# Rounding the bit-linear rows by a conversion to a scaled 16-bit float, with all five instruction orders written anew

## The reference, cut to what matters

```python
def bit_linear(x, w, b):
    gamma_x = jnp.clip(jnp.max(jnp.abs(x), axis=-1, keepdims=True), 1e-05, None)
    scale_x = 127.0 / gamma_x
    x_dq = jnp.clip(jnp.round(x * scale_x), -128.0, 127.0) / scale_x
    ...
    gamma_w = jnp.clip(jnp.mean(jnp.abs(w)), 1e-05, None)
    w_dq = jnp.clip(jnp.round(w / gamma_w), -1.0, 1.0) * gamma_w
    ...
    return jnp.einsum('bsd,hd->bsh', x_ste, w_ste) + b
gate = jax.nn.silu(bit_linear(x, gate_w, gate_b))
val = bit_linear(x, val_w, val_b)
return bit_linear(gate * val, out_w, out_b)
```

## Time and profile before

| what | value |
|---|---|
| time, median of 3 executions | 828.62 us (824.5 to 832.47) |
| span of the profiled execution | 828.8 us; its own time is not listed beside it |
| mean granted TensorE clock | 0.948 of full speed |
| instructions | 22129 |
| busy share PE / DVE / ACT / POOL | 92% / 89% / 84% / 77% |

### The profile page before, as it was taken

How to read it: one execution, slowest core, us unless ns; L and a number is a source line. 1 busy time by engine, 2 the same in 40 slices (tenths; PEclk the granted TensorE clock), 3 DMA queues, 4 the chain that set the end, 5 groups by cost and what they waited for, 6 DMA issues and landing times. The chain is left out here.

```text
span 828.8 us, 22129 instructions
## 1 busy us (share of the span) xinstructions
PE 759.6 (92%) x6898; PEld 397.6 (48%) x6898; DVE 739.1 (89%) x1636; ACT 699.6 (84%) x1447; POOL 636.2 (77%) x1139
## 2 busy tenths in 40 slices
...
GB/s 287 140 54 19 71 67 64 76 105 94 112 87 108 109 110 110 108 116 112 104 111 116 112 101 110 109 105 106 117 101 120 99 91 115 95 87 91 57 72 20
DMA packets 197952, 82.59 MB, mean 100 GB/s; under 512 B 139710, under 2 KB 196670, under 8 KB 197836
## 3 DMA queue, kind: packets, MB, share of 16 engines
...
## 5 line engine op out<-in xcount | busy, mean ns | idle before, releaser
L1141 DVE TENSOR_REDUCE mx<-psS 128x2 f32<-128x512 f32 x512 | 334.1, 680 | 21.8 <-PE psS L630 20.2
L813 ACT ACTIVATE prob<-psT 128x512 f32<-128x512 f32 x512 | 292.5, 604 | 27.0 <-PE psT L638 21.6
L630 PE MATMUL psS<-KQ 31*128 31x256 f16 x1024 | 137.6, 285 | 7.0 <-DVE mx L1141 3.6
L652 PE MATMUL psW<-prob,vst 128*32 128x256 f32 x2048 | 143.0, 400 | 0.1
L741 PE MATMUL psW<-guT,xT 128*128 128x512 bf16 x512 | 132.6, 387 | 6.2 <-DMA xT<-stage 5.3
L638 PE MATMUL psT<-KQ 32*128 32x256 f16 x1024 | 130.4, 280 | 4.0 <-ACT prob L813 3.1
L652 PEld LDWEIGHTS psW<-prob,vst 128*32 128x32 f32 x2048 | 55.0, 112 | 61.4 <-issue 34.6
L741 PEld LDWEIGHTS psW<-guT,xT 128*128 128x128 f16 x512 | 43.1, 99 | 71.5 <-issue 36.5
L1025 POOL TENSOR_TENSOR hqB<-wide,rnd 128x512 bf16<-128x512 f32 x60 | 63.1, 1056 | 13.6 <-ACT wide L863 13.4
L1039 POOL TENSOR_TENSOR stage<-stage 128x512 f16<-128x512 f32 x60 | 69.7, 1162 | 2.5 <-ACT stage L924 1.8
L630 PEld LDWEIGHTS psS<-KQ 31*128 31x128 f16 x1024 | 40.4, 93 | 64.2 <-DVE mx L1141 38.0
...
## 6 DMA issues: line engine op xcount, KB each, us to landing
...
xP<-in_x SPq DMA_DIRECT2D x32, 128.0 KB, 2.3
cP<-in_ctx SPq DMA_DIRECT2D x32, 128.0 KB, 2.1
xA<-in_x SPq DMA_DIRECT2D x32, 128.0 KB, 2.7
cB<-in_ctx SPq DMA_DIRECT2D x32, 128.0 KB, 2.3
oV<-uA SPq DMA_DIRECT2D x32, 128.0 KB, 2.1
out<-x SPq DMA_DIRECT2D x32, 128.0 KB, 2.0
...
```

The source lines that it names most:

```text
L630: m = nc.tensor.matmul(psS[:, n % 2, T * k:T * k + T], KQ[p % DEEP][r, 1, g, 128 * k:128 * k + 128], KQ[p % DEEP][r, 0, g, :], start=True, ...
L652: m = nc.tensor.matmul(bank[32 * j:32 * j + 32, :], vst[p % DEEP][:, k, 4 * n + j, :], prob[:, (4 * n + j) % 8, k, :], start=(k == 0), sto ...
L813: m = nc.scalar.activation(flat(prob[:, n % 8, :, :]), psT[:, n % 2, :], ACT.Exp, scale=float(HC) ** -0.5)
L1141: m = nc.vector.tensor_reduce(mx[:, p % 2, :, 4 * (n % 4) + n // 4], psS[:, n % 2, :].rearrange("p (c s) -> p c s", c=NK), AX.X, ALU.max)
```

## The change

- The scales become smaller by SUB = 2^24, and `xq` and `hr` write float16 (`xqB`, `hqB` are float16 now), so that ScalarE's conversion on the output does the rounding: a multiple of 2^-24. `xr` and both `hq` go, with the tiles `xrB`, `hrB` and `rnd`. The factor 2^24 comes back in the column scales.
- `tern` (the ternary weights), `xqT` and `hqT` are float16. The scale parts beside `xqB` stay bf16, through a second view `xrb`; the transposes of the last two pairs follow the types, and `lqc` becomes two copies.
- `hr` waits now for what `hq` waited for (the transpose of the pair before); `sxB` and `xnB` wait for `xq` where they waited for `xr`; `qT` and `ht` wait for `xq` and `hr`.
- All of `ORDER`, `HEAD` and `TAIL` is written anew; LOOP's bounds move by one or two. The banks are the same.

```diff
+SUB = 16777216.0
...
-    "pe": """ro:-5 pv0:-1 T6:-1 S8:0 T7:-1 bg0:-3 S9:0 proj0:2 Bg0:-3 S10:0 T8:-1 T9:-1 S11:0 pv1:-1 Bd:-4 bv0:-3
...
+    "pe": """S9:-3 pv0:-4 T8:-4 S10:-3 proj0:-1 bg0:-6 S11:-3 Bg0:-6 pv1:-4 S12:-3 T9:-4 T10:-4 Bd:-7 S13:-3 bv0:-6 Bv0:-6 bg1:-6
...
-LOOP = {"pe": (9, 26), "dve": (10, 26), "act": (10, 26), "pool": (9, 26), "sp": (9, 25)}
+LOOP = {"pe": (10, 26), "dve": (10, 26), "act": (10, 26), "pool": (10, 26), "sp": (10, 26)}
...
-        tern = [sb(f"tern{i}", [P, 2 * HID], BF16) for i in range(3)]
+        tern = [sb(f"tern{i}", [P, 2 * HID], F16) for i in range(3)]
...
-        xnB, xrB = sb("xnB", [P, T]), sb("xrB", [P, T])
-        xqB, xqT = sb("xqB", [P, T + P], BF16), sb("xqT", [P, NK + 1, P], BF16)
+        xnB = sb("xnB", [P, T])
+        xqB, xqT = sb("xqB", [P, T + P], F16), sb("xqT", [P, NK + 1, P], F16)
+        xrb, xrbT = xqB[:, T:T + P].bitcast(BF16), xqT[:, NK, :].bitcast(BF16)
...
-        hqB, hqT = sb("hqB", [P, HID], BF16), sb("hqT", [P, 8, P], BF16)
+        hqB, hqT = sb("hqB", [P, HID], F16), sb("hqT", [P, 8, P], F16)
...
                 elif name == "ht":
-                    after_apart(sp, "hq", p)
+                    after_apart(sp, "hr", p)
...
-                elif kind == "xr":
+                elif kind == "xq":
                     after(act, "sxB", p)
-                    after(act, "xq", p - 1)
-                    m = nc.scalar.activation(xrB[:], xnB[:], ACT.Copy, scale=sB[:, p % 2, 2:3], bias=ROUND)
-                elif kind == "xq":
-                    after(act, "xr", p)
                     after_late(act, p - 1, "lq", "qT")
-                    m = nc.scalar.activation(xqB[:, 0:T], xrB[:], ACT.Copy, bias=-ROUND)
+                    m = nc.scalar.activation(xqB[:, 0:T], xnB[:], ACT.Copy, scale=sB[:, p % 2, 2:3])
...
                 elif kind == "hr":
                     after(act, "sx", p)
-                    after(act, "hq", p - 1, n)
-                    m = nc.scalar.activation(hrB[:, 512 * n:512 * n + 512], hB[:, 512 * n:512 * n + 512], ACT.Copy,
-                                             scale=sB[:, p % 2, 8:9], bias=ROUND)
+                    after_late(act, p - 1, "lh", "ht", part=1)
+                    m = nc.scalar.activation(hqB[:, 512 * n:512 * n + 512], hB[:, 512 * n:512 * n + 512], ACT.Copy,
+                                             scale=sB[:, p % 2, 8:9])
...
-                elif kind == "hq":
-                    h = slice(512 * n, 512 * n + 512)
-                    after(pool, "hr", p, n)
-                    after_dma(pool, "ht", p - 1)
-                    m = nc.gpsimd.tensor_tensor(hqB[:, h], hrB[:, h], rnd[:].broadcast_to([P, 512]), ALU.subtract)
```

More of the change, by code:

```diff
@@ L72 @@
 DEEP = 3
-SET_POOL, SET_DVE = 13, DEEP + 3
+SET_POOL, SET_DVE = 12, DEEP + 3
 ORDER = {
-    "pe": """ro:-5 pv0:-1 T6:-1 S8:0 T7:-1 bg0:-3 S9:0 proj0:2 Bg0:-3 S10:0 T8:-1 T9:-1 S11:0 pv1:-1 Bd:-4 bv0:-3
[L76 to L89, removed]
```

413 lines of the change are left out of this document (212 added, 201 removed).

## The result

The changed kernel takes 889.3 us (median of 4 runs, 887.72 to 890.04), beside 828.05 us for the kernel before on the same chip: ratio 1.0715, 95% interval [1.0657, 1.0773]. I had forecast 856 us and a range from 838 to 871. Slower was right; the size was missed by 33 us. Executions of one kernel lie up to 2% apart, and the profile of three_merged, further down, is of its slowest (895.8 us, where the other three took 879.3 to 887.8).

The account below looks back on a forecast made before the run. PE and DVE bound the kernel before, PE alone after. From 828.8 us: +28.9 for pairs 5 to 25, +0.5 for pairs 26 to 30, 0 for the start, -1 for the end: 857, taken as 856, range 838 to 871.

Parts of the forecast that it names:

- PE bounds both kernels, and the change costs: Middle periods: PE and DVE both at their floor before; after, PE alone sets the period; slower 0.87.
- The price of groups: PE's score steps: 0.317 to 0.337 us a group of one to four; 16 groups for 8 cost 2.2 us a period.
- The rounding costs nothing on the path: ACT and POOL passes: xq's 13.5 us and hq's 63.1 us go, no gain from hr, operand types cost nothing.
- Neither sets the period, so none of this is on the path directly: ACT at some 19.8 and POOL at 17.1 us a period after the change, so their savings give nothing directly.
- earlier transposes: ht can start a hq (1.06 us) and a wait earlier; at most 0.77 us a period given back.
- The price of a period, 23.34 us: PE's summed distances for a period after, beside 21.16 before (21.36 measured).
- As a check I summed each instruction's undisturbed distance to its successor, by the kinds of both: PE's two orders: 21.16 us a period before, 23.34 after, difference 2.18, checking the 2.2 from groups.
- I leave 0.3 us a period: Late transfers left in each of 21 periods after the change, down from 0.77 us; bounds 0 and 0.8.
- each transfer has 2 us more per period to land: Argument in the middle periods against the rival that the new order brings new stalls.
- new stalls on top: Rival: PE's readers closer behind their transfers, lateness 0.8 or more a period, 21 x 0.6 more, 869 us; chance 0.13.
- others hold PE up there: Pairs 26 to 30: distances 106.8 before and 108.4 after, 113.5 measured before, so only +0.5 us.
- PE busy near 795 us: Sign that the forecast is right: PE's total busy time over the changed kernel.

Follow-up runs that it names:

- three_merged: Changed kernel with three pairs of neighbouring groups in PE's list of a period joined by the smallest moves (16 groups to 13): 884.29 us, ratio 1.0719.
- split_four: round_alone with four groups of four steps in PE's period each cut in two (8 groups to 12): 852.25 us, ratio 1.0278.
- round_alone: Changed kernel's code and rounding with the five lists of the kernel before, xq where xr stood and no hq: 817.98 us, ratio 0.9868.
- h_in_two_passes: round_alone with hB rounded in two passes again (ScalarE's hr adds 0.75, GpSimd's hq takes it off): 827.85 us, ratio 1.0005.
- bg0_last: round_alone with one exchange in PE's list of a period, bg0 behind S9 instead of ahead of it: 817.78 us, ratio 0.9875.
- Maxima_earlier: Changed kernel with the maxima's product ahead of Bv1 instead of behind it in PE's list of a period: 884.16 us, ratio 1.0714.
- merged_and_earlier: three_merged with the maxima's product also ahead of Bv1 in PE's list of a period: 879.04 us, ratio 1.0624.

## Why the prediction was right or wrong

- **PE bounds both kernels, and the change costs.** Right in sign. The price of groups is shown by split_four: 0.46 us for each added, come through in full, and by three_merged's shortest period: 0.38 for each taken away. The rule of the Trainium skill (TensorEngine Tiling (Array Packing), section Tiling Modes) that a change of mode drains the array prices only the way in and out, 0.22 us by the rows of before; the measurement is about twice that, since one step alone takes 0.31 us and four together 0.34. A lone S step is at 0.31 us as forecast, and in fast periods PE is busy throughout and DVE is not full.
- **The rounding costs nothing on the path.** Right that its price is small and that the conversion of small values isn't slow (`xq` 520 ns, `hr` 722 ns). ScalarE's pass was free, as said. "Neither sets the period, so none of this is on the path directly" left out a gain that GpSimd's pass does give under the old order: round_alone gains 1.3%, and h_in_two_passes loses it again. The prediction had named a way, earlier transposes, and a limit, 0.77 us a period; 0.34 came (22.13 to 21.79). POOL fell by 62 us as forecast, but ACT by 5 and not by 13: `xr`, `xq` and `hr` together are 15 us less by the rows, while the exponentials are busy for 298.4 us instead of 292.5; the other 4 us are not assigned.
- **The price of a period, 23.34 us.** Too low by 0.48: the fastest is 23.82, PE busy throughout. "As a check I summed each instruction's undisturbed distance to its successor, by the kinds of both" leaves out what stands ahead of an instruction, and several products are dearer behind a group. cP, the first half of a projection, is an instance. In the trace of before it takes 0.54 us behind the group of five and 0.43 behind another full product. In the changed kernel both cP stand behind groups, and the second, at 427.86, takes 0.54:

```profile
392.00 0.70 PE L665 MATMUL psW<-cP,wsm 128*128 128x256 f32 x2
392.54 0.59 PE L665 MATMUL psW<-xnP,wsm 128*128 128x256 f32 x2
...
399.14 0.59 PE L665 MATMUL psW<-cP,wsm 128*128 128x256 f32 x2
399.57 0.59 PE L665 MATMUL psW<-xnP,wsm 128*128 128x256 f32 x2
```

```profile
427.86 0.70 PE L668 MATMUL psW<-cP,wsm 128*128 128x256 f32 x2
428.40 0.59 PE L668 MATMUL psW<-xnP,wsm 128*128 128x256 f32 x2
```

v likewise takes 0.54 behind a group (412.90 to 413.44) where it took 0.45. Behind the two halves of xcT the next group starts after 0.59 us (434.98 to 435.57), where the order before had 0.53 (383.14 to 383.67). With ro, sc and Bg0, read in the same way, these make some 0.45 to 0.5, so nearly all of the 0.48. This is read from rows; no run moves one of these products alone. The distances of before also held a wait that is no price of PE's: S9's for its bank, which bg0_last shows and which is part of the 0.87 in the earlier trace rows. The check against 21.36 us was therefore weaker than it looked, because 21.36 is DVE's period as much as PE's. Over 21 periods the 0.48 are 10 us of the 33.
- **"I leave 0.3 us a period" of lateness.** This is the step that failed most. The fastest period is 23.82 and the mean 24.87, so 1.05 were left; over pairs 5 to 25, 520.1 us were measured against 496.8 forecast, and 13 of these 23 us are lateness. I argued from the slack of the other engines ("all other engines have 2 us and more in hand") and gave "each transfer has 2 us more per period to land" against the rival. Both look at the period; what counts is PE's work between a transfer's start and its reader, which the list fixes. Between the maxima's product and T0's group it is 3.8 us after where it was 5.0. In the 13 middle periods of the changed kernel whose records line up, PE's mean distances lie above the shortest by 0.46 us at T0's group, by 0.18 at the group of bv1, 0.16 ahead of bg0 and 0.10 ahead of y. Maxima_earlier took 0.47 off the mean period, as much as T0's share; merged_and_earlier brought more waits elsewhere as soon as PE was quicker. The rival that I named, new stalls on top (chance 0.13), is what happened. Its 869 us are 20 short all the same, as it took the period's price at 23.34; and 0.8 instead of 0.3 is 10.5 us over 21 periods, which makes 867, where it added 21 x 0.6.
- **Start +4.1 us, pairs 26 to 30 +3.4.** Forecast 0 and +0.5. The start is inside the bounds given, but round_alone starts 4.1 us faster than before (149.4 us, and the three others with its first pairs take 148.9 to 151.0), so the new first pairs cost some 8 us. No run took this apart; it stays open. Pairs 26 to 30 are 23.4 us a period, near PE's new price: "others hold PE up there" was no cover. The end was right (-0.6 for -1).
- **PE busy near 795 us.** It is 818.2. The distances that were too low are in it, and part of the waits: a matmul's end is modelled, so a short wait behind it can pass as busy time.

The better of all kernels run is round_alone, at 0.9868 of the time before: the rounding with the old order.
